# A state-space scan stage: the norm moved ahead of the next delta, preparation reordered, casts on ScalarE, the skip term on TensorE

## The chip, the cores and the metric

The kernel runs on one core of one Trainium2 chip. The metric is the device time of one execution in microseconds (us). Three runs of the kernel before gave 3763.31, 3771.71 and 3772.99 us, a median of 3771.71 us.

## The reference

Input: 16 sequences of 256 tokens with 128 features. `x = x + ssm(layernorm(x))` is followed by `x = x + ffn(layernorm(x))`, where `ssm` is a selective state-space block (256 inner channels, 16 states per channel) and `ffn` is itself six layers of windowed attention and a gated feed-forward part. Only the first line and the layer norm between the two are touched here (xn is the normalised input):

```
xz = xn @ W_in + b_in ; x_gate = xn @ W_gate + b_gate
act = silu(conv4(xz))                         # causal, depthwise
delta = softplus(act @ W_delta + b_delta)     # 256 channels
B, C = act @ W_B, act @ W_C                   # 16 numbers each, per token
h_t = exp(delta_t * A) * h_(t-1) + (delta_t * act_t) * B_t     # 256 channels x 16 states
y_t = sum_n h_t[n] * C_t[n] + act_t * D_skip
x1 = x + (y * silu(x_gate)) @ W_out + b_out
x2 = (x1 - mean(x1)) / sqrt(var(x1) + 1e-5)    # input of the attention part
```

## The kernel before, in words

Channels (or features) lie on the 128 partitions, tokens along the free dimension. The 4096 tokens are cut into 8 groups of 512 (two sequences each). The 256 inner channels make two halves, m = 0 and 1, so most things are done twice per group.

The scan stage is a loop over the groups. It is the body `scan_group`, written once per engine, with the first and the last group peeled off. Inside, n counts the 16 states. For each state and half (k = 2n + m):

- TensorE spreads row n of B over all partitions into PSUM bank 0 (`spread_b`, L1121), and row n of C into bank 1 (`spread_c`, L1125). The source is `bc_parts`, a bf16 tile that holds B and C in three parts (high, middle, low).
- VectorE multiplies `dx[m]` (delta times act) by bank 0 (L891, "product"); ScalarE makes the decay exp(delta·A) in bank 2 or 3 (L622); VectorE runs the recurrence (L897, "scan") on decay and product.
- ScalarE copies C to SBUF (L627, `c_sb`); GpSimd multiplies the state by it (L495, `hc`); TensorE adds that up over the states in bank 4 or 5 with an identity matrix (L1140).

Each engine runs its instructions in the order in which they are written; semaphores with counts tie the engines together. Between and beside the states lies the work that prepares group g+1 and finishes group g−1:

- TensorE: output product of g−1 in bank 7 at n = 2, 3; the four delta products of g+1 (banks 6 and 7) at n = 5 to 8; the two B/C products of g+1 (bank 6) at n = 13, 14; for the norm of g−1 the mean (L1111, bank 7) at n = 13, and the variance (L1115) at n = 15. The mean comes only after bank 7 has given up the delta of g+1.
- ScalarE: softplus of g+1 in eight pieces at n = 9 to 12 (`prepare`: L588 absolute value, L591 exponential, L594 positive part, L597 logarithm), each issued just ahead of a decay; square (L601) and root (L606, L608) of the norm near and after the end. Within one state its order is decay m = 0, copy of C, decay m = 1.
- VectorE: residual add of g−1 (L865) ahead of n = 5, centring of g−1 (L871) ahead of n = 14; after the last scan of the group `inputs(g+1)`: cast of B/C to bf16 (L831), the two deltas (L835), the rest r1 (L837), `dx[0]` (L839), the casts (L841, L842), r2 (L844), a cast (L846), `dx[1]` (L848). Then `gate(g)`: the skip term with D_skip added on VectorE (L856, twice) and the product with the gate (L860, twice); then the scaling of g−1 (L876).

After the last group, the attention stage starts as soon as the last norm is written; nothing of it is done earlier save loads and memsets.

Of the kernel before, what the change touches and what calls it, by code (L numbers as in the profile page):

```python
# [12 lines left out]
P = 128  # L13
# [89 lines left out]
def build(nc, t, out):  # L103
# [3 lines left out]
    with ctx:  # L107
# [119 lines left out]
        bc_parts = cut(GROUP // 2).bitcast(bf16)  # L227
        pxc, psq, prstd = (cut(GROUP) for _ in range(3))
# [54 lines left out]
        y_skip = sem("y_skip", MT)  # L283
# [61 lines left out]
        OUT_AT, D_AT, Z_AT, BC_AT, NORM_AT = 2, 5, 9, 13, 14  # L345
# [196 lines left out]
        def _(act_e):  # L542
            A = nc.scalar.activation
            give_credits(act_e, [c_kept, ln_log, p_log, act_done, f_ready, v_ready, tr_evac, o_evac] + in_used)
# [38 lines left out]
            def prepare(g, piece):  # L583

                step, m = divmod(piece, MT)
                if step == 0:
                    item(act_e, d_done, g * MT + m)
                    A(zabs[m], bank[6 + m][:], ACT.Abs, bias=mpar[:, m, B_DELTA:B_DELTA + 1]).then_inc(z_abs[0], 1)  # L588
                elif step == 1:
                    item(act_e, z_abs, g * MT + m)  # L590
                    A(zexp[m], zabs[m], ACT.Exp, scale=-1.0).then_inc(z_exp[0], 1)  # L591
                elif step == 2:

                    A(zpos[m], bank[6 + m][:], ACT.Relu, bias=mpar[:, m, B_DELTA:B_DELTA + 1]).then_inc(z_pos[0], 1)  # L594
# [15 lines left out]
            def scan_group(g, first, last):  # L610
                for k in range(D_STATE * MT):
                    n, m = divmod(k, MT)
                    b = k % NDA
                    if 0 <= k - Z_AT * MT < 4 * MT and not last:
                        prepare(g + 1, k - Z_AT * MT)
                    if k < MT:
                        item(act_e, delta_done, g * MT + m)

                    act_e.wait_ge(scan_done[0], g * (D_STATE * MT) + (k + 1 if k >= NDA else NDA))
                    d3 = delta[m].rearrange("p (s t) -> p s t", t=SEQ)  # L620
                    a3 = dA[b].rearrange("p (s t) -> p s t", t=SEQ)
                    A(a3[:, :, 1:], d3[:, :, 1:], ACT.Exp, scale=a_neg[:, m, n:n + 1]).then_inc(dA_done[0], 1)  # L622
                    if m == 0:
                        item(act_e, c_ready, g * D_STATE + n)
                        slot(act_e, hc0_done, g * D_STATE + n)
                        slot(act_e, hc1_done, g * D_STATE + n)
                        A(c_sb[n % 2], bank[1][:], ACT.Copy).then_inc(c_kept[0], 1)  # L627
                    if k == NORM_AT * MT + MT - 1 and not first:
                        square_of(g + -1)
                if not first:  # L630
                    root_of(g + -1)

            item(act_e, a_done, 1)
            for piece in range(4 * MT):
                prepare(0, piece)
# [145 lines left out]
        def _(dve):  # L781
            V = nc.vector
            give_credits(dve, [p_out, ln_xc, ln_out, bc_split, dbx_done, scan_done, y_skip, mo_used,
# [21 lines left out]
            V.tensor_scalar(a_neg, a_neg, -1.0, None, ALU.mult).then_inc(a_done[0], 1)  # L805

# [20 lines left out]
            def inputs(g):  # L827

                cols = ds(g * GROUP, GROUP)
                item(dve, bc_done, g)  # L830
                V.tensor_copy(bc_parts, bank[6][:]).then_inc(bc_step[0], 1)  # L831
                for m in range(MT):
                    item(dve, z_log, g * MT + m)
                    item(dve, z_pos, g * MT + m)
                    V.tensor_tensor(delta[m], zpos[m], zlog[m], ALU.add).then_inc(delta_done[0], 1)  # L835
                item(dve, bc_step, g * 4)
                V.tensor_tensor(r1, bank[6][:], bc_parts, ALU.subtract).then_inc(bc_step[0], 1)  # L837
                item(dve, delta_done, g * MT)
                V.tensor_tensor(dx[0], delta[0], act[0][:, cols], ALU.mult).then_inc(dx_done[0], 1)  # L839
# [5 lines left out]
                item(dve, bc_step, g * 4 + 3)  # L845
                V.tensor_copy(bc_parts[64:96], r2[64:96]).then_inc(bc_split[0], 1)  # L846
                item(dve, delta_done, g * MT + 1)
                V.tensor_tensor(dx[1], delta[1], act[1][:, cols], ALU.mult).then_inc(dx_done[0], 1)  # L848

            def gate(g):  # L850
# [7 lines left out]
                for m in range(MT):  # L858
                    item(dve, y_skip, g * MT + m)
                    V.tensor_tensor(gated[m], gated[m], sgate[m][:, cols], ALU.mult).then_inc(g_done[0], 1)  # L860

            def add_output(g):
# [3 lines left out]
                                       op0=ALU.add, op1=ALU.add).then_inc(mo_used[0], 1)  # L866

# [10 lines left out]
            def scan_group(g, first, last):  # L878
                for n in range(D_STATE):
                    if n == OUT_AT + 3 and not first:  # L880
                        add_output(g + -1)
                    if n == NORM_AT and not first:
                        centre_output(g + -1)
                    item(dve, b_ready, g * D_STATE + n)
                    for m in range(MT):
                        k = n * MT + m
                        if n == 0:
                            item(dve, dx_done, g * MT + m)
                        if k >= NH_BUF:
                            item(dve, scan_done, g * steps + (k - NH_BUF))  # L890
                        V.tensor_tensor(dbx[k % NH_BUF], dx[m], bank[0][:], ALU.mult).then_inc(dbx_done[0], 1)  # L891
                    for m in range(MT):
                        k = n * MT + m
                        item(dve, dA_done, g * steps + k)
                        item(dve, dbx_done, g * steps + k)
                        slot(dve, (hc0_done, hc1_done)[m], g * D_STATE + n)
                        V.tensor_tensor_scan(hst[k % NHC], dA[k % NDA], dbx[k % NH_BUF], 0.0, ALU.mult, ALU.add).then_inc(scan_done[0], 1)  # L897
                if not last:
                    inputs(g + 1)
                gate(g)  # L900
                if not first:
                    scale_output(g + -1)

            for n in range(NDA):
                item(dve, in_used[2 + n], GROUPS - 1)
                V.memset(dA[n].rearrange("p (s t) -> p s t", t=SEQ)[:, :, 0:1], 0.0).then_inc(dA_clear[0], 1)
            inputs(0)
# [131 lines left out]
        def _(pe):  # L1039
# [41 lines left out]
            def delta_product(g, m, k, after=None):  # L1081
# [3 lines left out]
                if m == 1 and k == 0 and after is not None:  # L1085
                    item(pe, mo_used, after)
# [30 lines left out]
            def scan_group(g, first, last):  # L1117
                def spread_b(n):

                    pe.wait_ge(dbx_done[0], g * steps + (n + 1) * MT)  # L1120
# [10 lines left out]
                for n in range(D_STATE + 1):  # L1131
                    if n + 1 < D_STATE:
                        spread_b(n + 1)
                    for m in range(MT):
                        k = (n - 1) * MT + m
                        if k >= 0:
                            item(pe, (hc0_done, hc1_done)[m], g * D_STATE + (n - 1))
                            if n == 1:
                                slot(pe, y_skip, g * MT + m)
# [4 lines left out]
                    if 0 <= n - OUT_AT < MT and not first:  # L1144
                        output_product(g + -1, n - OUT_AT, g, g + -1)
                    if 0 <= n - D_AT < MT * MT and not last:
# [280 lines left out]
```

## Time and profile before

| | value |
|---|---|
| median of 3 runs | 3771.71 us |
| profiled execution | 3762.99 us (span 3761.2 us) |
| VectorE busy, whole span | 3144.7 us, 84% |
| TensorE busy, whole span | 3503.5 us, 93% |
| ScalarE / GpSimd busy | 2644.4 us / 2424.0 us |
| granted TensorE clock, mean | 0.982 of full speed |

The page's 40 slices (94 us each) show TensorE at 6 to 7 tenths and VectorE at 8 to 9 tenths in the slices from 94 to 658 us, which is the scan stage, and TensorE at 9 tenths in all later ones, which is attention. The shares of the whole span are an average over these two stages and say little of either.

### The profile page before, as it was taken

How to read it: one execution, taken by the hardware profiler on the slowest of the kernel's cores; microseconds unless marked ns; L12 is line 12 of the kernel's file. 1: busy time of each engine (PE TensorE's matmuls, PEld its weight loads, DVE VectorE, ACT ScalarE, POOL GpSimd, SP SyncE). 2: the span in 40 equal slices, each digit the busy share in tenths (PEclk: the TensorE clock that was granted, in tenths of full speed). 3: DMA queues.
4: the chain of work that ended last, by engine and by line, in shares of the span. 5: the costliest groups of instructions: out<-in, count | busy, mean ns of one | idle time of the engine just before them, and what ended most of it. 6: DMA issues, size and time to landing. Idle time of an engine off the chain costs nothing.

```text
span 3761.2 us, 148676 instructions
## 1 busy us (share of the span) xinstructions
PE 3503.5 (93%) x61280; PEld 2220.5 (59%) x61280; DVE 3144.7 (84%) x4377; ACT 2644.4 (70%) x4969; POOL 2424.0 (64%) x2197
## 2 busy tenths in 40 slices
PE   6676776899999999999999999999999999999998
PEld 2222222566666666666666666666666666666665
DVE  6999998888888878888888888888888788888884
ACT  5554554677777777777777777777777777777775
POOL 0554554876766667766667676666666676667672
PEclk9899899999999999999999999999999999999999
DMA  3000000111111110111111111111111111111111
GB/s 79 1 0 0 0 0 0 32 32 32 32 43 43 38 33 29 34 46 38 38 33 32 43 43 35 31 32 32 49 38 37 30 31 43 43 38 32 32 32 39
DMA packets 64427, 120.20 MB, mean 32 GB/s; under 512 B 18196, under 2 KB 35986, under 8 KB 63634
## 3 DMA queue, kind: packets, MB, share of 16 engines
q1 hardware_dynamic: 63762, 110.70, 10.1%
q8 instruction: 494, 8.09, 0.9%
q14 instruction: 171, 1.40, 0.1%
HBM read 20.50 MB, written 2.10 MB: 6 GB/s over the span
## 4 chain that ended last, share of the span: by engine, by line
PE 79%; DVE 2%; issue 2%; ACT 1%; POOL 0%; POOLq 0%; DVEq 0%; ACTq 0%
PE qk L1186 17%; PE trb L1045 10%; PE ob L1247 10%; PE vob L1192 9%; PE vob L1255 8%; PE sc L1274 7%; PE sc L1223 6%; PE ob L1045 4%; PE sc L1281 3%; PE sc L1217 2%; PE vob L1297 1%; PE vob L1309 1%; DVE ssq L933 0%; DVE arena L927 0%; DVE arena L928 0%
## 5 line engine op out<-in xcount | busy, mean ns | idle before, releaser
L519 POOL TENSOR_TENSOR arena<-arena,rnorm 128x512 f32<-128x512 f32 x768 | 787.0, 1046 | 898.3 <-ACT rnorm L653 897.7
L512 POOL TENSOR_TENSOR arena<-arena 128x512 f32<-128x512 f32 x768 | 963.6, 1276 | 21.5 <-DVE arena L928 21.5
L1186 PE MATMUL qk<-wqkv,xs 128*128 128x512 f32 x1536 | 731.5, 599 | 17.9 <-issue 11.0
L660 ACT ACTIVATE arena<-trb 128x512 f32<-128x512 f32 x768 | 462.6, 602 | 405.5 <-PE trb L1045 405.4
L927 DVE TENSOR_TENSOR arena<-qk,tab_q 128x512 f32<-128x512 f32 x384 | 263.5, 686 | 413.1 <-ACT arena L646 405.6
L495 POOL TENSOR_TENSOR arena<-arena 128x512 f32<-128x512 f32 x256 | 300.3, 1182 | 339.8 <-DVE arena L897 329.1
L1045 PE MATMUL trb<-ident,arena 128*128 128x128 f32 x3076 | 484.1, 280 | 10.1 <-ACT arena L660 7.7
L1186 PEld LDWEIGHTS qk<-wqkv,xs 128*128 128x128 f32 x1536 | 292.8, 191 | 310.1 <-issue 292.4
L933 DVE TENSOR_REDUCE ssq<-arena 128x16 f32<-128x1024 f32 x384 | 463.9, 1208 | 0.0
L646 ACT ACTIVATE arena<-qk 128x512 f32<-128x512 f32 x768 | 426.4, 587 | 41.9 <-PE qk L1186 31.0
L1045 PEld LDWEIGHTS trb<-ident,arena 128*128 128x128 f32 x3076 | 347.8, 141 | 141.5 <-issue 95.8
L526 POOL TENSOR_TENSOR arena<-arena,rinv 128x512 f32<-128x512 f32 x384 | 393.0, 1045 | 27.1 <-DVE rinv L950 27.1
L1247 PE MATMUL ob<-arena 64*64 64x32 f32 x24576 | 397.4, 220 | 0.0
L1247 PEld LDWEIGHTS ob<-arena 64*64 64x64 f32 x24576 | 376.2, 135 | 34.0 <-issue 34.0
L1192 PE MATMUL vob<-wqkv,xs 128*128 128x512 f32 x768 | 394.0, 594 | 0.5 <-DVE arena L990 0.4
L1255 PE MATMUL vob<-arena,wo 128*128 128x256 f32 x1536 | 363.8, 380 | 1.3 <-ACT arena L683 0.7
L1255 PEld LDWEIGHTS vob<-arena,wo 128*128 128x128 f32 x1536 | 276.8, 190 | 31.6 <-issue 1.9
L1223 PEld LDWEIGHTS sc<-arena 64*32 64x32 f32 x24576 | 278.8, 105 | 16.2 <-issue 5.9
L1223 PE MATMUL sc<-arena 64*32 64x64 f32 x24576 | 283.0, 225 | 4.3 <-issue 4.3
L1274 PE MATMUL sc<-xnT,w 128*128 128x512 f32 (+1 forms) x576 | 272.1, 595 | 8.9 <-DVE xnT L1017 7.5
L667 ACT ACTIVATE arena<-vob 128x512 f32<-128x512 f32 x384 | 232.9, 607 | 50.7 <-PE vob L1192 50.6
L927 DVE TENSOR_TENSOR arena<-qk,tab_k 128x512 f32<-128x512 f32 x384 | 261.6, 681 | 4.0 <-ACT arena L646 3.7
(155 smaller groups left out, 5848.1 us busy)
## 6 DMA issues: line engine op xcount, KB each, us to landing
arena<-arena SPq DMA_DIRECT2D x192, 384.0 KB, 3.2
arena<-arena SPq DMA_DIRECT2D x192, 64.0 KB, 3.0
wqkv<-in_L_ffn_Wqkv SPq DMA_DIRECT2D x18, 512.0 KB, 3.8
wo<-in_L_ffn_Wo SPq DMA_DIRECT2D x6, 512.0 KB, 5.6
arena<-in_L_attn_x SPq DMA_DIRECT2D x8, 256.0 KB, 4.7
out<-arena SPq DMA_DIRECT2D x8, 256.0 KB, 2.2
w<-in_L_ffn_W SPq DMA_DIRECT2D x6, 341.0 KB, 3.2
arena<-in_sel SPq DMA_DIRECT2D x1, 1024.0 KB, 4.9
```

The costliest lines, as they stand in the source:

```text
L512: nc.gpsimd.tensor_tensor(ts[c * 2 + j][:, heads], tu[:, 0, heads], tu[:, 1, heads], ALU.add).then_inc(summed[0], 1)
L519: nc.gpsimd.tensor_tensor(part, part, rnorm[j][:, 8 * h:8 * h + 8].unsqueeze(2).to_broadcast([P, 8, HEAD]), ALU.mult) \
L660: A((qT, kT)[j][u][:, 4 * h:4 * h + 4, at_col:at_col + P], TRB.rearrange("p (a t) -> p a t", a=4), ACT.Copy) \
L927: V.tensor_tensor(tu[:, 0, heads], src, tab[:, c, 0:1, :].to_broadcast([P, 8, HEAD]), ALU.mult)
L933: V.tensor_reduce(ssq[j][:], sq[j].rearrange("p (h e) -> p h e", h=HEADS), op=ALU.add, axis=AX.X).then_inc(ssq_done[0], 1)
L1045: return MM(out_, lhsT=in_, rhs=ident[0:k, 0:k], is_transpose=True, **kw)
L1186: MM(QK[:, 512 * h:512 * h + 512], lhsT=xs[u][:, c * P:(c + 1) * P], rhs=wqkv[:, col:col + 512], start=True, stop=True) \
L1192: MM(VOB[:, :], lhsT=xs[u][:, c * P:(c + 1) * P], rhs=wqkv[:, col:col + STEP_COLS], start=True, stop=True).then_inc(vproj_done[0], 1)
L1223: last = MM(SC[32 * g:32 * g + 32, col:col + SPAN], lhsT=qT[u][d, STEP_PAIRS * j + a, t0:t0 + WINDOW], rhs=kT[u][d, STEP_PAIRS * j + a, t0 ...
L1247: last = MM(OB[d, col:col + WINDOW], lhsT=v[keys, g // 2, (2 * a + h) * HEAD:(2 * a + h + 1) * HEAD], rhs=probT[keys, h, a, g * WINDOW:(g ...
L1255: last = MM(VOB[:, 0:SEQ], lhsT=wo[:, STEP_PAIRS * j + a, :], rhs=oT[:, a, :], start=a == 0, stop=a == STEP_PAIRS - 1)
L1274: MM(SC[0:hn, 512 * b:512 * b + 512], lhsT=w1[:, col:col + hn], rhs=rhs, start=True, stop=True).then_inc(up_done[0], 1)
```

## The change

What it does, by engine:

- **TensorE.** Output product of g−1 at n = 0, 1; mean of g−1 at n = 3, variance at n = 6; delta products of g+1 at n = 2 and 4 (bank 6) and at n = 8 and 9 (bank 7, now after the root of g−1 has read that bank); B/C products at n = 10, 11. Two new products per group, at n = 5 and 7, add act·D_skip to banks 4 and 5 through a diagonal matrix `skip[m]`.
- **ScalarE.** Order within a state: decay m = 1, copy of C, then decay m = 0 of the next state. The softplus pieces stand at n = 5, 9, 11, 13 ahead of the decay m = 1 of states 6, 10, 12, 14; the last logarithm after state 15. Square and root of g−1 at n = 5 and n = 7. The three casts of B/C (`split`) are done here. The first decay of a group waits for one scan fewer.
- **VectorE.** Residual add ahead of n = 3, centring ahead of n = 5. The two deltas of g+1 come before the last scan of g, after a wait for the last decay. `inputs` keeps r1, both `dx` and r2 (now of 32 partitions with low rows first). The scaling of g−1 comes before `gate`, and `gate` is one multiplication per half that reads PSUM. Once, before the convolution, two 128x128 multiplications make `skip[m]`.

```diff
+        skip = [cut(P) for _ in range(MT)]
-        OUT_AT, D_AT, Z_AT, BC_AT, NORM_AT = 2, 5, 9, 13, 14
+        ADD_AT, CENTRE_AT = 3, 5
+        OUTPUT = {0: 0, 1: 1}
+        DELTA = {2: (0, 0), 4: (0, 1), 8: (1, 0), 9: (1, 1)}
+        MEAN_AT, VAR_AT = 3, 6
+        SKIP = {5: 0, 7: 1}
+        BC = {10: 0, 11: 1}
+        PIECES = {5: ((Z_ABS, 0),), 9: ((Z_POS, 0), (Z_EXP, 0)), 11: ((Z_LOG, 0), (Z_ABS, 1)), 13: ((Z_POS, 1), (Z_EXP, 1))}
+        SQUARE_AT, ROOT_AT = 5, 7
...                                                     (ScalarE)
+            def split(g):
+                item(act_e, bc_done, g)
+                A(bc_parts, bank[6][:], ACT.Copy).then_inc(bc_step[0], 1)
+                item(act_e, bc_step, g * 4 + 1)
+                A(bc_parts[0:64], r1[0:64], ACT.Copy).then_inc(bc_step[0], 1)
+                item(act_e, bc_step, g * 4 + 3)
+                A(bc_parts[0:32], r2[0:32], ACT.Copy).then_inc(bc_split[0], 1)
...
+                decay(0, 0)
+                decay(0, 1)
+                keep_c(0)
+                decay(1, 0)
+                for n in range(1, D_STATE, 2):
+                    decay(n, 1)
+                    keep_c(n)
+                    if n + 1 < D_STATE:
+                        decay(n + 1, 0)
+                        if not last:
+                            for piece, m in PIECES.get(n, ()):
+                                prepare(g + 1, piece, m)
+                        if n == SQUARE_AT and not first:
+                            square_of(g + -1)
+                        if n == ROOT_AT and not first:
+                            root_of(g + -1)
+                        decay(n + 1, 1)
+                        keep_c(n + 1)
+                        decay(n + 2, 0)
+                if not last:
+                    prepare(g + 1, Z_LOG, 1)
+                    split(g + 1)
...                                                     (VectorE)
             def inputs(g):
-                item(dve, bc_done, g)
-                V.tensor_copy(bc_parts, bank[6][:]).then_inc(bc_step[0], 1)
                 item(dve, bc_step, g * 4)
                 V.tensor_tensor(r1, bank[6][:], bc_parts, ALU.subtract).then_inc(bc_step[0], 1)
-                item(dve, bc_step, g * 4 + 1)
-                V.tensor_copy(bc_parts[32:64], r1[32:64])
-                V.tensor_copy(bc_parts[64:P], r1[64:P]).then_inc(bc_step[0], 1)
+                for m in range(MT):
+                    item(dve, delta_done, g * MT + m)
+                    V.tensor_tensor(dx[m], delta[m], act[m][:, cols], ALU.mult).then_inc(dx_done[0], 1)
                 item(dve, bc_step, g * 4 + 2)
-                V.tensor_tensor(r2[64:96], r1[64:96], bc_parts[64:96], ALU.subtract).then_inc(bc_step[0], 1)
-                V.tensor_copy(bc_parts[64:96], r2[64:96]).then_inc(bc_split[0], 1)
+                V.tensor_tensor(r2[0:32], r1[0:32], bc_parts[0:32], ALU.subtract).then_inc(bc_step[0], 1)
...
-                    V.scalar_tensor_tensor(out=gated[m], in0=act[m][:, cols], scalar=mpar[:, m, D_SK:D_SK + 1], in1=bank[4 + m][:],
-                                           op0=ALU.mult, op1=ALU.add).then_inc(y_skip[0], 1)
-                    V.tensor_tensor(gated[m], gated[m], sgate[m][:, cols], ALU.mult).then_inc(g_done[0], 1)
+                    V.tensor_tensor(gated[m], bank[4 + m][:], sgate[m][:, cols], ALU.mult).then_inc(g_done[0], 1)
...
+                if not last:
+                    item(dve, dA_done, g * steps + (steps - 1))
+                    deltas(g + 1)
+                scan_of(g, D_STATE - 1, MT - 1)
                 if not last:
                     inputs(g + 1)
-                gate(g)
                 if not first:
                     scale_output(g + -1)
+                gate(g)
...                                                     (TensorE)
-                    item(pe, mo_used, after)
+                    item(pe, p_log, after)
...
+                    if n in SKIP:
+                        m = SKIP[n]
+                        MM(bank[4 + m][:], lhsT=skip[m], rhs=act[m][:, ds(g * GROUP, GROUP)], start=False, stop=False)
```

## Rows read from the trace of the kernel before

**Rows 1.** Windows: the scan stage; busy us of each engine, then clock, DMA.

```profile
97.00:645.00 548.00, 381.99 (x911) 147.22 (x909) 521.62 (x643) 282.74 (x463) 300.31 (x256) 0.92 0.00 0
```

**Rows 2.** Line L601, scan stage: shapes, count | busy us, mean ns | idle before, releaser.

```profile
L601 ACT ACTIVATE arena<-arena 128x512 f32<-128x512 f32 x7 | 4.4, 629 | 8.0 <-DVE arena L871 8.0
```

**Rows 3.** Waits of VectorE, 103 to 642 us: total us, times, longest.

```profile
DVE arena L871 <- PE ob L1111: 12.3, 7, 1.9
DVE arena L897 <- ACT trb L622: 10.2, 15, 1.4
```

**Rows 4.** Timeline, VectorE: first products of groups 0 and 7 (start, us).

```profile
103.88 1.28 DVE L891 TENSOR_TENSOR arena<-arena,qk 128x512 f32<-128x512 f32 x2
...
582.98 1.27 DVE L891 TENSOR_TENSOR arena<-arena,qk 128x512 f32<-128x512 f32 x2
```

**Rows 5.** Timeline, VectorE: last state of group 2 and the boundary behind it.

```profile
293.62 1.26 DVE L891 TENSOR_TENSOR arena<-arena,qk 128x512 f32<-128x512 f32 x2
...
295.93 1.20 DVE L897 TENSOR_TENSOR_SCAN arena<-trb,arena 128x512 f32<-128x512 f32 x1
297.05 0.66 DVE L831 CAST arena<-ob 128x512 bf16<-128x512 f32 x1
297.63 1.82 DVE L835 TENSOR_TENSOR arena<-arena 128x512 f32<-128x512 f32 x2
299.37 0.68 DVE L837 TENSOR_TENSOR arena<-ob,arena 128x512 f32<-128x512 f32 x1
...
300.68 0.42 DVE L841 CAST arena<-arena 32x512 bf16<-32x512 f32 x1
...
301.57 0.68 DVE L844 TENSOR_TENSOR arena<-arena 32x512 f32<-32x512 f32 x1
...
302.74 0.69 DVE L848 TENSOR_TENSOR arena<-arena 128x512 f32<-128x512 f32 x1
...
303.34 1.40 DVE L856 SCALAR_TENSOR_TENSOR arena<-arena,sc 128x512 f32<-128x512 f32 x2
304.66 0.68 DVE L860 TENSOR_TENSOR arena<-arena,xT 128x512 f32<-128x512 f32 x1
...
305.87 0.68 DVE L876 TENSOR_TENSOR xT<-arena 128x512 f32 x1
```

**Rows 6.** GpSimd beside VectorE: line L835 (min/median/max), and two stretches of timeline.

```profile
L835 DVE TENSOR_TENSOR arena<-arena x16: 677/683/1222, 98.6 to 575.3; 128x512 f32<-128x512 f32 x16
...
296.09 2.21 POOL L495 TENSOR_TENSOR arena<-arena 128x512 f32<-128x512 f32 x2 [0.92 <-DVE arena L897]
...
1121.65 2.22 POOL L519 TENSOR_TENSOR arena<-arena,rnorm 128x512 f32<-128x512 f32 x2 [3.47 <-ACT rnorm L653]
1121.74 1.24 DVE L1017 TENSOR_SCALAR xnT<-arena,lpar 128x512 f32<-128x512 f32 x1
```

**Rows 7.** Windows in group 2; TensorE's timeline: sums of one state, first spread of group 3.

```profile
236.00:240.00 4.00, 0.74 (x2) 0.19 (x2) 4.00 (x7) 0.12 (x1) 0.00 (x0) 0.50 0.00 0
...
248.00:256.00 8.00, 6.86 (x18) 2.56 (x16) 8.00 (x10) 3.92 (x8) 5.20 (x5) 1.00 0.00 0
...
285.72 1.88 PE L1140 MATMUL sc<-arena,ident 128*128 128x512 f32 x4
...
302.84 0.39 PE L1121 MATMUL qk<-arena 128*128 128x512 bf16 x1 [3.36 <-DVE arena L846]
```

**Rows 8.** Timeline: start of the scan stage, and the end of its last group.

```profile
96.42 1.15 ACT L597 ACTIVATE arena<-arena 128x512 f32<-128x512 f32 x2
...
98.03 0.69 DVE L831 CAST arena<-ob 128x512 bf16<-128x512 f32 x1 [10.71 <-PE ob L1094]
...
642.90 0.75 DVE L856 SCALAR_TENSOR_TENSOR arena<-arena,sc 128x512 f32<-128x512 f32 x1 [1.34 <-PE sc L1140]
643.95 0.75 DVE L856 SCALAR_TENSOR_TENSOR arena<-arena,sc 128x512 f32<-128x512 f32 x1 [0.30 <-PE sc L1140]
...
647.44 0.75 DVE L865 SCALAR_TENSOR_TENSOR x1T<-ob,arena,x1T 128x512 f32<-128x512 f32 x1 [0.94 <-PE ob L1105]
```

More of the change, by code:

```diff
@@ L610, in scan_group, with decay @@
             def scan_group(g, first, last):
[L611 to L616, printed above, removed]
+                def decay(n, m):
+                    k = n * MT + m
+                    if n == 0:
                         item(act_e, delta_done, g * MT + m)
-                    act_e.wait_ge(scan_done[0], g * (D_STATE * MT) + (k + 1 if k >= NDA else NDA))
+                    act_e.wait_ge(scan_done[0], g * (D_STATE * MT) + (k + 1))
@@ L628, in scan_group, with keep_c @@
[L628 to L631, printed above, removed]
+                def keep_c(n):
+                    item(act_e, c_ready, g * D_STATE + n)
+                    slot(act_e, hc0_done, g * D_STATE + n)
+                    slot(act_e, hc1_done, g * D_STATE + n)
+                    A(c_sb[n % 2], bank[1][:], ACT.Copy).then_inc(c_kept[0], 1)
+                decay(0, 0)
+                decay(0, 1)
@@ L805, in _ @@
             V.tensor_scalar(a_neg, a_neg, -1.0, None, ALU.mult).then_inc(a_done[0], 1)
+            dve.wait_ge(ident_in[0], 16)
+            for m in range(MT):
+                V.tensor_scalar(skip[m], ident[:], mpar[:, m, D_SK:D_SK + 1], None, ALU.mult).then_inc(skip_made[0], 1)
             def conv_group(g):
@@ L825, in _, with deltas @@
             steps = D_STATE * MT
-            def inputs(g):
-                cols = ds(g * GROUP, GROUP)
-                item(dve, bc_done, g)
-                V.tensor_copy(bc_parts, bank[6][:]).then_inc(bc_step[0], 1)
+            def deltas(g):
                 for m in range(MT):
@@ L866, in add_output, with products_of, scan_of @@
                                        op0=ALU.add, op1=ALU.add).then_inc(mo_used[0], 1)
+            def products_of(g, n):
+                item(dve, b_ready, g * D_STATE + n)
+                for m in range(MT):
+                    k = n * MT + m
+                    if n == 0:
+                        item(dve, dx_done, g * MT + m)
+                    if k >= NH_BUF:
+                        item(dve, scan_done, g * steps + (k - NH_BUF))
+                    V.tensor_tensor(dbx[k % NH_BUF], dx[m], bank[0][:], ALU.mult).then_inc(dbx_done[0], 1)
+            def scan_of(g, n, m):
+                k = n * MT + m
+                item(dve, dA_done, g * steps + k)
+                item(dve, dbx_done, g * steps + k)
+                slot(dve, (hc0_done, hc1_done)[m], g * D_STATE + n)
+                V.tensor_tensor_scan(hst[k % NHC], dA[k % NDA], dbx[k % NH_BUF], 0.0, ALU.mult, ALU.add).then_inc(scan_done[0], 1)
             def centre_output(j):
@@ L879, in scan_group @@
                 for n in range(D_STATE):
-                    if n == OUT_AT + 3 and not first:
+                    if n == ADD_AT and not first:
                         add_output(g + -1)
-                    if n == NORM_AT and not first:
+                    if n == CENTRE_AT and not first:
                         centre_output(g + -1)
[L884 to L897, printed above, removed]
+                    products_of(g, n)
+                    scan_of(g, n, 0)
+                    if n < D_STATE - 1:
+                        scan_of(g, n, MT - 1)
+                if not last:
+                    item(dve, dA_done, g * steps + (steps - 1))
+                    deltas(g + 1)
+                scan_of(g, D_STATE - 1, MT - 1)
                 if not last:
                     inputs(g + 1)
-                gate(g)
                 if not first:
                     scale_output(g + -1)
+                gate(g)
             for n in range(NDA):
```

64 lines of the change are left out of this document (28 added, 36 removed).

## Prediction, on record before the run

> **What bounds the kernel now.** The page alone misleads: over the span TensorE is busiest, because attention takes most of it. I cut the scan stage out with the view of windows. There VectorE is busy 521.6 of 548 us, TensorE 382, ScalarE 283 and GpSimd 300 [rows 1]. Attention starts only after the last norm of this stage, so what the stage loses the whole execution loses, one for one. Then I read VectorE's timeline of one group. A state is two products and two scans: from 293.62 to 297.05, that is 3.43 us, without a gap [rows 5], and sixteen make 54.85 us. But from the first product of group 0 to that of group 7 there are 582.98 − 103.88 = 479.1 us [rows 4], or 68.4 per group. The other 13.6 us are the subject. The waits of VectorE name two causes: its centring waits for the mean on TensorE (12.3 us in 7 groups), and its scans wait for decays (10.2 us, 15 times) [rows 3]. The rest is VectorE's own work at the boundary: from the cast at 297.05 to the end of the scaling at 305.87 + 0.60 = 306.47 are 9.42 us [rows 5]. So VectorE's queue is the bound, and the question is which of its instructions and waits go, and whether another engine is then late.
>
> **The boundary.** I take distances between starts, since an instruction's recorded time overlaps the next by about 0.08 us: an ordinary 128x512 operation costs 0.60 us (304.66 for two of L860, then 305.87: 0.605 each), r1 0.61, a scan 1.12 to 1.13 (295.93 to 297.05) [rows 5].
>
> Gone from VectorE: the cast L831, 297.05 to 297.63, 0.58; casts L841 and L842 with the wait before r2, 300.68 to 301.57, 0.89; of r2 and the last cast, 301.57 to 302.74 = 1.17, all but the 0.60 of r2, so 0.57; the skip term L856 twice, 303.34 to 304.66, 1.32; the wait of 0.1 behind `dx[0]`. Together 3.46. Fewer partitions make nothing cheaper: r2 on 32 partitions is recorded with 0.68, as the full tiles [rows 5].
>
> What remains: deltas 1.20, r1 0.61, two dx 1.20, r2 0.62, scaling 0.60, gate 1.20 = 5.43 us.
>
> To this comes GpSimd. Before, the two deltas take 1.82 recorded and 1.74 in starts, where 1.20 is plain work [rows 5]; one of each pair takes up to 1.22 us where the least is 0.68 [rows 6]. That is when GpSimd's second multiplication is running: 296.09 + 2.21 = 298.30, and 297.63 + 1.22 − 0.60 is 298.25. So a VectorE operation with two SBUF inputs stands still until GpSimd's is nearly over, some 0.96 us after that one's start at 296.09 + 1.10 = 297.19. Afterwards two places are exposed. (a) Deltas: they now follow scan m = 0 of state 15, at whose end GpSimd starts its multiplication (0.16 us after VectorE's next start: 296.09 against 295.93). Delta 0 gets in first; does GpSimd get in before delta 1? At 1121.65 two GpSimd operations take 2.22 and L1017, issued at 1121.74, takes 1.24 [rows 6]: it ended at 1122.98, after the first and well before the second was over, so the port changes hands between two operations of one engine. I take this as the rule here: delta 1 loses 0.96. Bounds: 0 (both deltas back to back) and 1.10 (a whole multiplication). (b) `dx[0]` starts 0.61 after the scan's successor, GpSimd at 0.16 holds until 1.12: 0.51 lost; bounds 0 and 1.10.
>
> The Trainium skill says the same of the mechanism ("SBUF — State Buffer", section "Who interferes with whom"): an operation of VectorE with two SBUF inputs contends with a reading GpSimd one, and whoever is first holds the shared port for the whole instruction; a PSUM input does not contend. By that, the gate reading PSUM and the scans stay free, as the trace's scans show, but moving the deltas beside a live multiplication is a cost of this change. The page does not say who is next when both wait; no row shows it for two VectorE instructions.
>
> Sum: 5.43 + 0.96 + 0.51 = 6.90 per boundary, against 9.42.
>
> **Is anything late in its place?** T = start of r1. `dx[0]` waits to 1.12, `dx[1]` from 1.73, r2 from 2.33 and ends about 3.0. ScalarE's last cast (0.63, like L601 [rows 2]) follows to 3.7; the B spread takes 0.39 at full clock [rows 7]; at half its 0.21 of columns double, so 0.6; some 0.15 to start: 4.2 to 4.45. VectorE meanwhile does scaling and gate until 4.74 and then needs bank 0. So the casts, 0.6 to 0.7 us each, are hidden with 0.3 to 0.5 us to spare. Before, the spread came at 302.84 [rows 7], 3.6 us early; this cover is used up. ScalarE's first two casts have room: r1's successor is ready 0.7 + 0.65 after T, before `dx[1]` ends. The last logarithm and the first cast lie between the last decay and delta 1, where ScalarE has 2.3 us after scan m = 1 of state 14 for four operations of 0.6 to 0.7 us, of which delta needs three. The first decay of g+1 follows the split at about 4.4, its scan is at 4.74 + 1.2: free.
>
> **Inside the states.** The mean now has two states between the residual add (n = 3) and the centring (n = 5), about 7 us for a 0.94 us product behind some 4 us of queue: the wait of 12.3 us goes. Scans wait for a decay because decay m = 1 stands behind the copy of C, which waits for TensorE's spread; at a group's start TensorE runs at half clock (0.50 from 236 to 240, 1.00 from 248 on [rows 7]), and an output product stands in its queue. In the new order decay m = 1 comes first, so the copy has until the next scan m = 0. Softplus pieces: after scan m = 0 of an even step ScalarE does decay, two pieces, decay: 0.69 + 2·0.65 + 0.69 = 2.7 us, while VectorE needs the last 3.44 us after that scan. Slack 0.7. TensorE carries 12 extra products per group rather than 10 (skip term), now one per state. The sums of a state are four passes in 1.88 us [rows 7]; an extra product is two such passes, 0.94; the two spreads add less than 0.39 each: under 3.6 with every tail counted, and the tails overlap, so some 3.1 of 3.43 us. I take both waits as gone; bounds: gone, or 2 us per group kept.
>
> **The sum.** Groups 0 to 6: 7·54.85 + 6·1.25 (residual add 0.64, centring 0.61) + 7·6.90 − 0.60 (nothing to scale in group 0) = 439.2 against 479.1: 39.9 us. Group 7, first product to last scan: 582.98 to 642.90 − 1.34 = 641.56 [rows 4, 8] is 58.5; 54.85 + 1.25 remain: 2.4. Its end: the scaling fills the 1.34 us of waiting before the gate, the gate is done 0.60 after the last sum (643.95), near 644.6, instead of 645.8, so the residual add at 647.44 [rows 8] comes about 1.6 earlier (bounds 0 and 2.4). Start: from the first cast at 98.03 [rows 8] to the first product at 103.88 were 5.85; now from the last logarithm (96.42 + 1.15 = 97.57 [rows 8]): cast, deltas in its shade, r1, two dx, r2, cast, spread: 0.7 + 0.7 + 1.2 + 0.7 + 0.7 + 0.6, some 4.6: 1.7 earlier (bounds 0 and 2.2). The two multiplications for `skip` (128x128, 0.2 us) lie before a convolution that waits for ScalarE anyway: nothing, at most 0.5. Total 45.6 us.
>
> The profiled execution took 3762.99 us (span 3761.2), so its like comes to 3717.4. The median of the three runs is 8.7 above the profiled one and its lowest 0.3 above; I take half of that offset: **3722 us**.
>
> **Rivals.**
> - *The deltas pass together.* GpSimd does not get in between; 7 times 0.96 less, so 3715. For: VectorE starts an instruction before the former ends. Against: L1017's handover [rows 6].
> - *The split chain ends last.* The chain r2, ScalarE, spread has 0.3 to 0.5 us of slack by my count; with one longer hop, or the copy's decays late, VectorE waits about 1 us per boundary: 7 boundaries, 3729.
> - *It doesn't do what it says.* Pieces of ScalarE's work that are issued in pairs make the scans wait instead: seven states of a group with 0.7 us of slack; if each missed it by 0.6, 4.2 per group, 34 us, which leaves 12: 3756. Against: the pieces were issued one per decay before and only a few of the waits fall there.
> - *Slower: TensorE stays at half clock.* The end of each group (n = 12 to 15) is now bare of extra products. If the clock did not come back at the group's start, a state's sums would cost near 2·1.8 = 3.6 us on TensorE, with the spreads over 4.2, with an extra product 5.9, against 3.43. From about four such states with an extra product per group (10 us, against 5.7 saved) it loses; with six, 15 us in each of 8 groups against 46 saved, 3790. For: clock 0.50 at each start [rows 7]. Against: it is back by 248, within three states [rows 7], and the stage's mean of 0.92 [rows 1] leaves half clock for only 16% of it, though four states of each group were bare before too; also the idle of TensorE at the boundary shrinks and the output product follows at n = 0.
>
> **How the numbers follow.** Forecast 0.50, together 0.20, split chain 0.18, paired pieces 0.07, half clock 0.05. Range: from the second case with its start and end terms at their better bounds, 3706, to the third with 2 us of waits per group kept, 3742. What can be told from no change is 0.3%, 11 us. The first three cases are faster by more, and half of the fourth: 0.91; same 0.05; slower 0.04.
>
> **What would show it.** Period between first products of inner groups 63.0 us (61.9 to 64); no wait of L871 and at most a few tenths for the scans; deltas with one of the pair near 1.6 us and GpSimd's multiplication of state 15 late by 0.4; `dx[0]` near 1.2; first product not waiting for the spread. Wrong if VectorE waits at n = 0 for TensorE's B, if scans wait for L622's successor at even states, or if the granted clock stays at 0.50 past n = 3.

## The result, and the profile after

The kernel after takes 3717.65 us in the median of 4 runs (3717.34 to 3724.26); the kernel before 3769.47 us (4 runs, 3763.31 to 3772.99). The ratio is 0.9868, with a 95% interval of 0.9851 to 0.9886. Forecast were 3722 us with 3706 to 3742, and 3717.4 for a profiled execution; that one took 3717.34 us. So close a total is partly luck, as the terms below show: some missed upwards and others downwards by as much.

All distances below are from one profiled execution of each kernel. The norm before attention (L876 before, L923 after) starts at 653.43 us before and at 610.05 us after, 43.4 us earlier. The rest of the span is 3107.8 us before and 3105.5 us after; that stage is not touched by the change, and in a second profiled execution of the same kernel after it took 3109.4 us. So I read the change in the scan stage, whose seven periods sum to 439.75 and 439.18 us in these two executions, not in the total.

VectorE's timeline of the kernel after: the first products of groups 0 and 7. They answer to [rows 4].

```profile
103.51 1.29 DVE L906 TENSOR_TENSOR arena<-arena,qk 128x512 f32<-128x512 f32 x2 [1.36 <-PE qk L1163]
...
543.26 1.26 DVE L906 TENSOR_TENSOR arena<-arena,qk 128x512 f32<-128x512 f32 x2
```

That is 439.75 us for seven periods, where it was 479.1 and 439.2 were forecast. The waits of VectorE in this stage (us in total, times, longest) answer to [rows 3]:

```profile
DVE arena L890 <- PE sc L1182: 4.1, 3, 2.6
DVE x1T L895 <- PE ob L1147: 2.5, 3, 1.2
DVE arena L906 <- PE qk L1163: 1.7, 2, 1.4
DVE arena L918 <- PE ob L1153: 1.2, 1, 1.2
```

No scan waits for a decay any more, and a centring (L918) waits for the mean only once, behind the last group, as it did before. New inside the groups are waits for TensorE: the gate (L890) once, 2.61 us; the residual add (L895) twice, 0.66 and 0.61 us; the first product (L906) once, 0.34 us. The rest of these rows belongs to the start and the end of the stage (1.36 us for the product, twice 0.74 for the gate, 1.22 for the add).

The boundary behind group 1, all engines, answers to [rows 5] and [rows 7]:

```profile
220.69 2.16 DVE L871 TENSOR_TENSOR arena<-arena 128x512 f32<-128x512 f32 x2
220.85 1.45 POOL L504 TENSOR_TENSOR arena<-arena 128x512 f32<-128x512 f32 x1 [0.92 <-DVE arena L913]
...
222.78 1.21 DVE L913 TENSOR_TENSOR_SCAN arena<-trb,arena 128x512 f32<-128x512 f32 x1
...
223.91 0.66 DVE L877 TENSOR_TENSOR arena<-ob,arena 128x512 f32<-128x512 f32 x1
224.06 1.09 POOL L504 TENSOR_TENSOR arena<-arena 128x512 f32<-128x512 f32 x1 [1.76 <-DVE arena L913]
224.49 1.81 DVE L880 TENSOR_TENSOR arena<-arena 128x512 f32<-128x512 f32 x2
...
226.22 0.67 DVE L882 TENSOR_TENSOR arena<-arena 32x512 f32<-32x512 f32 x1
226.83 0.67 DVE L923 TENSOR_TENSOR xT<-arena 128x512 f32 x1
226.93 0.63 ACT L614 ACTIVATE arena<-arena 32x512 bf16<-32x512 f32 x1 [1.70 <-DVE arena L882]
227.43 0.67 DVE L890 TENSOR_TENSOR arena<-sc,xT 128x512 f32<-128x512 f32 x1
...
227.69 0.60 PE L1163 MATMUL qk<-arena 128*128 128x512 bf16 x1 [1.36 <-ACT arena L614]
228.03 0.67 DVE L890 TENSOR_TENSOR arena<-sc,xnT 128x512 f32<-128x512 f32 x1
...
228.63 1.26 DVE L906 TENSOR_TENSOR arena<-arena,qk 128x512 f32<-128x512 f32 x2
```

From r1 at 223.91 to the next product at 228.63 are 4.72 us; 4.74 were forecast. The two deltas take 2.09 from start to start (220.69 to 222.78); 2.16 were forecast. ScalarE's last cast begins at 226.93, TensorE's spread of B ends at 228.29, 0.34 us before the product that needs it. The casts are hidden, just.

The boundary behind group 3 is another thing. Deltas, GpSimd, both dx, both gates and TensorE's last sum:

```profile
345.56 1.25 DVE L871 TENSOR_TENSOR arena<-arena 128x512 f32<-128x512 f32 x2
345.70 2.06 POOL L504 TENSOR_TENSOR arena<-arena 128x512 f32<-128x512 f32 x1 [0.92 <-DVE arena L913]
...
348.02 3.86 POOL L504 TENSOR_TENSOR arena<-arena 128x512 f32<-128x512 f32 x1 [0.26 <-DVE arena L913]
348.45 1.27 DVE L880 TENSOR_TENSOR arena<-arena 128x512 f32<-128x512 f32 x2
...
349.65 0.67 DVE L882 TENSOR_TENSOR arena<-arena 32x512 f32<-32x512 f32 x1
350.25 0.67 DVE L923 TENSOR_TENSOR xT<-arena 128x512 f32 x1
...
350.86 0.67 DVE L890 TENSOR_TENSOR arena<-sc,xT 128x512 f32<-128x512 f32 x1
...
351.94 2.07 PE L1182 MATMUL sc<-arena,ident 128*128 128x512 f32 x2 [2.99 <-POOL arena L504]
...
354.13 0.69 DVE L890 TENSOR_TENSOR arena<-sc,xnT 128x512 f32<-128x512 f32 x1 [2.61 <-PE sc L1182]
```

Here both deltas pass together, and so do both dx, r2 and the scaling. GpSimd's multiplication, 1.09 us when alone, takes 3.86: it ends at 351.88, 1.0 us after the gate (one input from PSUM) has begun. Below I call such a multiplication starved. TensorE's sum comes late and at half clock (2.07 us for what takes 1.13 elsewhere), and the gate of half 1 waits 2.61 us. Before, no multiplication of this stage took over 1.29 us.

### The profile page after: what moved, and what is told of

Read it like the earlier page. It is cut to its first block, busy times and chain, and to the rows that moved or that the text cites. A ratio compares the mean times of both kernels' runs of the same rounds, so it can differ in the third digit from the quotient of the medians.

```text
span 3715.5 us, 148691 instructions
## 1 busy us (share of the span) xinstructions
PE 3532.4 (95%) x61312; PEld 2227.1 (60%) x61312; DVE 3117.0 (84%) x4331; ACT 2658.2 (72%) x4993; POOL 2428.3 (65%) x2197
## 3 DMA queue, kind: packets, MB, share of 16 engines
q14 instruction: 168, 1.37, 0.1%
## 4 chain that ended last, share of the span: by engine, by line
PE 81%; DVE 2%; issue 1%; ACT 1%; POOL 0%; DVEq 0%; ACTq 0%; POOLq 0%
PE qk L1230 17%; PE trb L1087 10%; PE ob L1291 10%; PE vob L1299 9%; PE vob L1236 9%; PE sc L1318 7%; PE sc L1267 7%; PE ob L1087 4%; PE sc L1325 3%; PE sc L1261 2%; PE vob L1341 1%; PE vob L1353 1%; DVE arena L969 0%; DVE arena L970 0%; DVE ssq L975 0%
## 5 line engine op out<-in xcount | busy, mean ns | idle before, releaser
L1087 PE MATMUL trb<-ident,arena 128*128 128x128 f32 x3076 | 485.8, 280 | 11.3 <-ACT arena L696 7.3
L1267 PEld LDWEIGHTS sc<-arena 64*32 64x32 f32 x24576 | 277.9, 105 | 14.1 <-issue 3.3
L1182 PE MATMUL sc<-arena,ident 128*128 128x512 f32 x512 | 259.8, 626 | 24.3 <-POOL arena L504 23.3
```

Source lines behind the costliest of these rows:

```text
L1087: return MM(out_, lhsT=in_, rhs=ident[0:k, 0:k], is_transpose=True, **kw)
L1267: last = MM(SC[32 * g:32 * g + 32, col:col + SPAN], lhsT=qT[u][d, STEP_PAIRS * j + a, t0:t0 + WINDOW], rhs=kT[u][d, STEP_PAIRS * j + a, t0 ...
```

## The experiments

Each kernel has its own profiled execution. "Periods" are distances between first scans of successive groups. In the kernel after they are 61.45, 63.66, 61.98, 64.17, 62.90, 63.60, 61.98; in the kernel before 64.73 and then 68.5 to 70.2.

**One part alone: the norm moved ahead** (on the kernel before).

```diff
-        OUT_AT, D_AT, Z_AT, BC_AT, NORM_AT = 2, 5, 9, 13, 14
+        OUTPUT = {0: 0, 1: 1}
+        DELTA = {2: (0, 0), 4: (0, 1), 8: (1, 0), 9: (1, 1)}
+        MEAN_AT, VAR_AT, ADD_AT, CENTRE_AT, SQUARE_AT, ROOT_AT = 3, 6, 3, 5, 5, 7
+        Z_AT, BC_AT = 10, 13
...                                                     (the engines' bodies use these)
```

> The kernel before with one part of the change: output product at n = 0, 1, mean and variance at n = 3 and 6, centring at n = 5, square and root at n = 5 and 7, delta products at 2, 4, 8, 9, softplus pieces one state later; casts, skip term, deltas and the order decay, copy, decay as before. My theory (VectorE's queue is the bound): the wait of the centring goes, 7 x 1.96 = 13.7 us less than 3763, and of the scan waits (10.2 us) some stay because a decay still stands behind the copy of C: 3742 to 3750. Rival (the wait only moves): TensorE at half clock makes the residual add at n = 3 or the decays late by as much as was gained: 3758 or more.

Measured: 3748.29 us, ratio to before 0.9944 (0.9927 to 0.996). Seven periods shrink from 479.1 to 465.0, by 14.1 (13.7 expected, for the centring). The centring waits no more inside the groups (11.3 us in these periods before), and the scans wait 3.2 us less than before. What is left of their waits for the decay behind the copy of C:

```profile
DVE arena L900 <- ACT trb L625: 7.0, 11, 1.3
```

So this part brings its 14 us by itself. In the kernel after, which has decay m = 1 ahead of the copy, the 7.0 us are gone too. That the order does it fits, but no run has the order alone.

**One part undone: the skip term** (on the kernel after).

```diff
-                    V.tensor_tensor(gated[m], bank[4 + m][:], sgate[m][:, cols], ALU.mult).then_inc(g_done[0], 1)
+                    V.scalar_tensor_tensor(out=gated[m], in0=act[m][:, cols], scalar=mpar[:, m, D_SK:D_SK + 1], in1=bank[4 + m][:],
...
+                    V.tensor_tensor(gated[m], gated[m], sgate[m][:, cols], ALU.mult).then_inc(g_done[0], 1)
...
-                        MM(bank[4 + m][:], lhsT=skip[m], rhs=act[m][:, ds(g * GROUP, GROUP)], start=False, stop=False)
```

> The kernel after with the skip term back on VectorE (two operations of 0.66 us per group, two TensorE products fewer). Theory: all of it is on VectorE's path: 8 x 1.32 = 10.6 us slower than after, near 3728. Rival: the gate waits for TensorE's last sum anyway, so the two operations fill a wait: no change, 3717.

Measured: 3731.04 us (0.9892, 0.9875 to 0.9908). From the last scan of a group to the first of the next: 8.37 us against 7.04, so 1.33 per boundary; the seven periods grow by 10.5. The skip term was wholly on the path. Its 7 × 1.33 are 9.3 of the 10.5; the rest is a mixture, for in this run no multiplication is starved, while all seven pairs of deltas take 2.16 or 2.17 us and the residual add waits in more groups.

**One part undone: the casts.**

```diff
...                                                     (ScalarE)
-                    split(g + 1)
...                                                     (VectorE)
+                V.tensor_copy(bc_parts, bank[6][:]).then_inc(bc_step[0], 1)
...
+                V.tensor_copy(bc_parts[0:64], r1[0:64]).then_inc(bc_step[0], 1)
...
+                V.tensor_copy(bc_parts[0:32], r2[0:32]).then_inc(bc_split[0], 1)
```

> The kernel after with the three casts of B and C back on VectorE (0.58 + 0.43 + 0.45 us and about 0.2 of waits between dependent operations). Theory: 7 boundaries x 1.7 = 11.6 us slower than after, near 3729. Rival (the split chain through ScalarE ends last in after): the chain gets shorter here by some 0.5 us, so that VectorE loses less than the casts cost: under 3722.

Measured: 3726.7 us (0.9878, 0.9862 to 0.9895), less than expected. The boundary is 1.09 us longer (8.13), not 1.7, and the periods 6.6 in all (7 × 1.09 would be 7.6, but no multiplication is starved here). The reason stands in its timeline:

```profile
223.34 0.65 DVE L877 CAST arena<-ob 128x512 bf16<-128x512 f32 x1
224.03 0.69 DVE L879 TENSOR_TENSOR arena<-ob,arena 128x512 f32<-128x512 f32 x1
224.64 1.28 DVE L882 TENSOR_TENSOR arena<-arena 128x512 f32<-128x512 f32 x2
```

The cast fills the time in which GpSimd multiplies, so the dx behind it take 1.28 instead of 1.81 us. Taking the cast away from VectorE moved dx into a collision; of the gain of 1.6 half a microsecond was given back to it. The forecast of the whole change had both as terms of their own; what I expected of this run had forgotten the second.

**The collision itself.** GpSimd's two multiplications of state 15 on 8 of 512 columns:

```diff
+                        w = GROUP if n < D_STATE - 1 else 8
...
+                        nc.gpsimd.tensor_tensor(hc[k % NHC][:, 0:w], hst[k % NHC][:, 0:w], c_sb[n % 2][:, 0:w], ALU.mult) \
...
```

The other 504 columns are left out of the computation; the run is for its times only.

> The kernel after; GpSimd's two multiplications of state 15 work on 8 of the 512 columns (part of the computation left out). Theory (port): nothing collides at the boundary: the pair of deltas takes 1.26 us in every group instead of 2.16 in most, the pair of dx 1.27 instead of 1.81, no wait of the gate: 4 x 0.9 + 6 x 0.54 + 2.6, some 8 to 10 us faster than after, near 3709. Rival (the second operation is long for another reason, a semaphore between dependent operations or a late logarithm): times of deltas and dx as before, 3717.

Measured: 3708.15 us (0.9843, 0.9822 to 0.9863). Periods 59.81 and then six times 61.46 or 61.47. One boundary, and all seven are alike:

```profile
217.94 1.27 DVE L872 TENSOR_TENSOR arena<-arena 128x512 f32<-128x512 f32 x2
...
220.85 1.28 DVE L881 TENSOR_TENSOR arena<-arena 128x512 f32<-128x512 f32 x2
```

The long deltas and dx, the gate's wait inside the groups, and the steps in the periods are all gone with GpSimd's columns, so GpSimd's multiplications caused them. The seven periods are 11.2 us shorter than in after. That is more than the 8 to 10 expected, because the residual adds no longer wait either (1.27 us); TensorE's sums come earlier here, so this part need not be the port. 61.46 is VectorE's bare work: 54.85 + 1.25 + 5.43 = 61.53 by the terms of the prediction.

**The same kernel again.**

> The kernel after once more, to see which parts of its stage repeat. Theory: all operations of VectorE repeat to 0.1 us save who gets the shared port behind the first delta; so the periods of the groups take few values (62.0 where both deltas pass together, about 62.9 where GpSimd gets in, 64 where GpSimd is starved and the last sum is late), in another order than before. Total 3715 to 3725. Rival: the periods scatter without such steps.

Measured: 3719.36 us (0.9869, 0.9848 to 0.989). Periods 61.45, 63.46, 61.99, 64.19, 62.89, 62.00, 63.20. The starved multiplication is behind group 3 again (3865 ns); behind groups 5 and 6 the two cases have changed places. So behind groups 0 to 4 the outcome was the same in both executions, and later not; what decides it these runs don't show.

**Deltas behind the last scan.**

```diff
-                if not last:
-                    item(dve, dA_done, g * steps + (steps - 1))
-                    deltas(g + 1)
                 scan_of(g, D_STATE - 1, MT - 1)
+                if not last:
+                    deltas(g + 1)
```

> The kernel after with the two deltas behind the last scan of the group instead of before it. Theory (port): deltas and dx then all fall beside one GpSimd multiplication rather than two, so one of the two blocks per boundary goes (0.5 to 0.9 us where it happened): 2 to 6 us faster than after, 3712 to 3716, with the multiplication of state 15, m = 1, at up to 4 us where it is starved. Rival (the order of need is what gained): the first decay and the spread come later and VectorE waits at the first product or scan of a group, 3717 or more.

Measured: 3716.54 us (0.9858, 0.9841 to 0.9874); periods 60.72, then 62.36 or 62.37 four times, 63.17 and 63.08. 436.4 us in all, 3.3 less than after.

```profile
282.09 2.59 POOL L504 TENSOR_TENSOR arena<-arena 128x512 f32<-128x512 f32 x2 [0.92 <-DVE arena L913]
283.06 2.17 DVE L871 TENSOR_TENSOR arena<-arena 128x512 f32<-128x512 f32 x2
...
285.75 1.28 DVE L880 TENSOR_TENSOR arena<-arena 128x512 f32<-128x512 f32 x2
```

One collision instead of two, and none starved. Putting the deltas ahead of the last scan, as the change does, gained nothing: nobody waits for an early delta, since ScalarE's first decay stands behind its own casts.

**Deltas before both scans of state 15.**

```diff
...                                                     (ScalarE)
+                    if n == D_STATE - 1 and not last:
+                        prepare(g + 1, Z_LOG, 1)
                     decay(n, 1)
...                                                     (VectorE)
                     products_of(g, n)
+                    if n == D_STATE - 1 and not last:
+                        item(dve, dA_done, g * steps + (steps - 1))
+                        deltas(g + 1)
                     scan_of(g, n, 0)
...
```

> The kernel after with both deltas before both scans of state 15 (and the last logarithm before the last decay). There GpSimd is at the end of state 14's second multiplication. Theory (port): delta 0 loses 0.3 us, delta 1 nothing, dx as in after (0.5): 0.3 instead of 0.9 in most groups and no starved multiplication: 2 to 4 us faster than after, 3712 to 3716. Rival (ScalarE decides): the logarithm ahead of the last decay makes a scan of state 15 wait, 3718 or more.

Measured: 3716.79 us (0.9862, 0.9841 to 0.9883). Periods 60.58, 62.25, 62.22, 62.99, then three of 62.2; VectorE's deltas and dx in one boundary, alike in all:

```profile
218.30 1.52 DVE L872 TENSOR_TENSOR arena<-arena 128x512 f32<-128x512 f32 x2
...
222.57 1.81 DVE L881 TENSOR_TENSOR arena<-arena 128x512 f32<-128x512 f32 x2
```

The deltas lose 0.26 instead of 0.90, as expected. The seven periods sum to 434.7 against 439.7: 5.0 less. The total doesn't show this; the attention stage, which the edit does not touch, took longer in this execution (span less the start of the norm: 3111.2).

**Residual add one state later, skip matrices behind the convolution.**

```diff
-        ADD_AT, CENTRE_AT = 3, 5
+        ADD_AT, CENTRE_AT = 4, 5
...                                                     (the two operations for skip move behind the convolution)
```

> The kernel after with two small edits: the two multiplications for skip go behind the convolution, where VectorE waits some 10 us for the first logarithm; the residual add of g-1 goes from n = 3 to n = 4. Theory: the convolution starts 0.8 us earlier, and the add no longer waits for the output product while TensorE is at half clock (2.5 us in 3 groups): 3 us faster, near 3714. Rival for the add: the product with B of the next state then waits for the mean on TensorE, and the wait only moves: 3717.

Measured: 3720.73 us (0.987, 0.9848 to 0.9892): no gain. The add no longer waits inside the groups, but a product does, for B, since TensorE's output product stands ahead of that spread:

```profile
176.20 1.29 DVE L903 TENSOR_TENSOR arena<-arena,qk 128x512 f32<-128x512 f32 x2 [0.28 <-PE qk L1163]
```

0.28 where the add had waited 0.66 in the same group. In group 4, where no add had waited, a product waits 0.67. And the start of the stage scatters between executions of one kernel by more than the 0.8 us that I had put down to the skip matrices: VectorE has finished the convolution at 88.03 and 89.65 us in the two of the kernel after, at 89.66 here. That they cost anything is not shown. This run had two starved multiplications, so its periods are longer in spite of the edit.

**Two combinations.** Deltas behind, add at n = 4, skip late:

> The kernel after with the deltas behind the last scan (as in the run before with that edit), the residual add at n = 4 and the multiplications for skip behind the convolution. Theory: the pair of deltas takes 2.17 us and the pair of dx 1.28 in every group, no starved multiplication, period 62.4 us in all inner groups; up to 0.4 us less in the groups in which the add waited: some 3 us faster than after, 3714 to 3717. Rival: the later add makes products wait for B, period above 62.6, no gain over after.

Measured: 3715.12 us (0.9865, 0.9849 to 0.9881), periods 436.5 in all, as without the two further edits.

Everything with two SBUF inputs moved out of GpSimd's way, and the gate of half 1 into the next group:

```diff
                     products_of(g, n)
...
+                        deltas(g + 1)
+                        delta_act(g + 1)
+                        rest_one(g + 1)
                     scan_of(g, n, 0)
+                    if n == 0 and not first:
+                        gate(g + -1, (1,))
...
+                    rest_two(g + 1)
                 scan_of(g, D_STATE - 1, MT - 1)
...
+                gate(g, range(MT) if last else (0,))
```

> The kernel after with VectorE's boundary work spread so that nothing with two SBUF inputs stands beside a running GpSimd multiplication save the tail of one: deltas, both dx and r1 between the products and the scans of state 15, r2 between its scans, the scaling of g-1 between product and scan of state 9, the gate of half 1 after the first scan of the next group, residual add at n = 4, skip matrices behind the convolution. Theory: the period is its work, 54.85 + 1.25 + 5.43 and 0.3 to 0.4 of port waits = 61.8 to 61.9 us in every inner group, against 61.98 to 64.2 in after: 7 to 9 us faster than after, 3708 to 3712. Rival: ScalarE's split, whose second cast now stands between the last decay and the first of the next group, or TensorE's spread of B with the new place of the gate, makes VectorE wait at the first product or scan of a group; then 62.5 or more and no gain over the variant with the deltas behind.

Measured: 3735.81 us (0.9918, 0.9904 to 0.9932), some 18 us slower than after; periods 62.6, then 65.1 to 65.7. (`delta_act` is the two dx, `rest_one` r1, `rest_two` r2. The scaling, the residual add and the operations for skip move too.)

```profile
226.84 0.65 DVE L883 TENSOR_TENSOR arena<-arena 32x512 f32<-32x512 f32 x1
227.00 1.46 POOL L504 TENSOR_TENSOR arena<-arena 128x512 f32<-128x512 f32 x1 [4.16 <-DVE arena L915]
...
228.50 3.68 PE L1193 MATMUL sc<-arena,ident 128*128 128x512 f32 x4 [4.49 <-POOL arena L504]
...
230.68 0.69 DVE L892 TENSOR_TENSOR arena<-sc,xT 128x512 f32<-128x512 f32 x1 [2.05 <-PE sc L1193]
...
232.54 1.29 DVE L908 TENSOR_TENSOR arena<-arena,qk 128x512 f32<-128x512 f32 x2 [1.17 <-PE qk L1174]
```

VectorE's own work has no long collision left, but the scans of state 15 come 3.3 us later. TensorE idles 4.49 us, begins at half clock (3.68 us for four passes that took 1.88 in [rows 7]), and the gate of half 0, which now follows at once, waits for it 2.05 us. The spread of B stands behind both sums, and the product waits another 1.17. The work that I had taken away from behind the last scan was the cover of that chain.

No version that computes everything beats the kernel after by more than the intervals. Deltas behind, or before both scans, are 3 to 5 us better in the scan stage by their traces; their totals (3716.5 and 3716.8) agree with after's (3717.65 and 3719.36) within their runs.

## Why the prediction was right, step by step

| term | forecast | measured |
|---|---|---|
| groups 0 to 6, less | 39.9 | 479.1 − 439.75 = 39.35 |
| group 7, first product to last scan, less | 2.4 | 58.6 − 56.1 = 2.5 |
| its end, last scan to residual add, less | 1.6 | 5.9 − 4.7 = 1.2 |
| start, first product earlier | 1.7 | 0.4 |
| after the residual add and in attention, less | 0 | 2.3 |

In the first row, too, two misses cancel: the deltas lost 3.1 us less than the 6.7 given to them, and waits that stood in no term (2.61 at the gate, 1.27 at the residual adds, 0.34 at the first product) cost 4.2. That the sum came within 0.6 us is luck; that it was near 440 is not.

The first two rows are the sum of one idea: VectorE's queue is the bound, so each operation that goes counts with its distance, and each wait with its row. The parts bear it out one by one: norm ahead 14.1, skip term 10.5, casts 6.6, and 8.2 of the 39.35 is left. The decays ahead of the copy fit it (7.0 us of waits were left when the norm alone was moved), but it is a remainder, not a run, and holds what the undoing of each part changed in the collisions as well.

Wrong inside the right sum:

- *Delta 1 loses 0.96 in each boundary.* The pair of deltas took 2.15 to 2.17 in four boundaries of seven and 1.25 or 1.26 in three. So the handover that I read from L1017 [rows 6] holds sometimes: 0.90 where it happens. The rival "the deltas pass together" has the other three. It was not worth the 0.96 each that I gave it, for one of those three brought the starved multiplication and a wait of 2.61 us.
- *`dx[0]` loses 0.51:* 1.81 against 1.27, so 0.54, in six of seven. The exception is the starved one.
- *Both waits inside the states are gone.* Those of the decays and of the centring are. But the output product, now at n = 0 and 1, runs when TensorE is at half clock, and the residual add waited 0.6 to 0.7 us in two groups. I had given TensorE's slack only at full clock. In those two groups, 1 and 5, the granted clock was still 0.79 and 0.85 in the stretch from 8 to 12 us after the first scan of the group, in the others 0.99 or 1.00.
- *The split chain has 0.3 to 0.5 us to spare:* 0.34 in the boundary shown. Behind group 0, where no scaling stands between, the first product waited 0.34 us. The case "split chain ends last" is right there and nowhere else.
- *Start and end.* The start term fell short of its sum: from the end of the convolution (87.26 before, 88.03 after) to the first product are 16.6 and 15.5 us, 1.1 less of 1.7, and the stage began 0.8 later, which scatters anyway. The chain that I had added up was right: from the end of the last logarithm (97.79 + 1.15 = 98.94) to the first product are 4.57 us, 4.6 were forecast. But that logarithm ends 1.37 us later than before, and I had taken its time over unchanged; 0.6 of it falls between the convolution and the logarithm, where five of the eight delta passes of TensorE took 1.06 us or more, four before. At the end I had taken the scaling as free, since it fills a wait. But it runs beside GpSimd's last multiplication, which takes 1.47 us instead of 1.10, and TensorE's last sum then starts 1.60 us behind the last scan instead of 1.23, and the gate behind it.

```profile
598.35 2.59 POOL L504 TENSOR_TENSOR arena<-arena 128x512 f32<-128x512 f32 x2 [0.92 <-DVE arena L913]
599.32 0.67 DVE L923 TENSOR_TENSOR xT<-arena 128x512 f32<-128x512 f32 x1
...
600.99 1.12 PE L1182 MATMUL sc<-arena,ident 128*128 128x512 f32 x2 [0.37 <-POOL arena L504]
```

- *Two sums of the prediction don't come out of their own terms.* The lower bound of 3706: 3722 less 6.7 for the deltas, 0.5 and 0.8 for the better start and end is 3714. And the price of the rival on half clock: 15 us in each of 8 groups less the 46 saved is 74 us slower, near 3840, not 3790. The forecast of 3722 rests on neither.

GpSimd and the pair of dx behind group 3: the multiplication that began at 348.02 ended only after VectorE's operations that began from 348.45 on, and the gate with a PSUM input runs at 0.67 us beside it. The Trainium skill ("SBUF — State Buffer", section "Who interferes with whom") says that VectorE and GpSimd contend where VectorE has two SBUF inputs; the traces agree, deltas and dx lose time and the gate doesn't. It also says that the order of issue decides who blocks. With 3.86 us for the multiplication that began first by its recorded start, this case does not show it so: by that rule dx would have waited, as it did in six boundaries of seven, and not the multiplication.

## What to carry to other kernels

Where one engine's in-order queue is full, price an edit by the distances between starts in its own timeline; the sum held to 0.6 us in 440, if partly by luck. What such a sum cannot hold is whom a removed operation had kept apart: look at what runs on GpSimd at that moment, and at which chain on TensorE the removed work had covered. Work behind the last scan was worth keeping there, since something had to stand between it and the gate.

## What the runs showed of the hardware that was not expected

- A GpSimd multiplication of 1.09 us took 1.45, 2.06 or 3.86 us with one, two or four VectorE operations of two SBUF inputs beside it (a delta; both deltas; two dx, r2 and the scaling); VectorE lost 0.90, 0 and 0. Who is next when both wait changed between two executions of the same kernel at the same place.
- The two passes of one sum took 1.13 us in most boundaries at a granted clock of 1.00. They took 2.07 us at 0.50 after 2.99 us without a matmul, and four took 3.68 us, nearly all at 0.50, after 4.49 us of idling. The length of the gap alone does not tell which: in the second execution of the kernel after, two sums came after 1.73 us each, one at half clock behind group 0 and one at full clock behind group 1.

```profile
162.52 2.08 PE L1182 MATMUL sc<-arena,ident 128*128 128x512 f32 x2 [1.73 <-POOL arena L504]
...
225.79 1.12 PE L1182 MATMUL sc<-arena,ident 128*128 128x512 f32 x2 [1.73 <-POOL arena L504]
```
